# Self attentions of a four-layer decoder: keys and queries split and stacked through DRAM, one fp32r product of scores for four heads, half batches in one pipeline

## The chip, the core and the metric

The kernel is written for one NeuronCore of a Trainium2 chip. The metric is the device time of one execution in microseconds (us), as the median of several executions. The engines are named as in the profile: PE is TensorE (its weight loads are PEld), DVE is VectorE, ACT is ScalarE, POOL is GpSimd, and SP is SyncE, which issues the DMAs.

## What is computed

A decoder of four layers works on 16 batches of 100 tokens with 128 features; each layer is a self attention, a cross attention over 1444 context rows and a feed-forward block. The change concerns the four self attentions alone. Layer 1's is the plainest:

```python
q, k, v = split(x @ w_attn.T)                 # 16 heads of 8 features each
att = einsum('bhqd,bhkd->bhqk', q, k) / sqrt(8)
att = where(causal, att, -inf); att = softmax(att)
y = einsum('bhqk,bhkd->bhqd', att, v)
x = x + y @ w_proj.T
```

Layer 0 has biases, a temperature of 0.1 and a gate for each token, a clipped sigmoid that multiplies the attention's output. Layer 2 is a differential attention: two softmaxes a head (q1, k1 and q2, k2), whose outputs are subtracted with a factor lambda, values 16 wide, an RMS norm for each head, and no causal mask. Layer 3 divides the 8 features of each head of q and of k by their norm before the scores.

## The kernel before

x lies in SBUF with features on the 128 partitions and the 1600 tokens in the free dimension; xn is its layer norm. There are four groups of four batches (`NG`, `GB`; `GT` is 400 tokens). Each engine has a program of its own, in the order of the stages: self attention, cross attention and feed-forward, with layer norms between them. The order within an engine is that of the code; engines wait for each other by semaphores.

`self_attention(n)` loops over the four groups, and the loop's turns do not overlap. Each turn has three parts.

First the preparation: DVE copies the group to `xg` (L1552), PE makes q and k for 400 tokens in fp32 (L2509), ACT copies them to `qk`, and PE makes the values (L2526 adds the bias row, L2527 is the product), which ACT writes to `vaug` with a column of ones beside each head. A head has 8 of the 128 partitions, so for the scores the keys are masked: `km` holds 16 copies of the keys, one for each head, with all other heads' features set to zero. ACT makes five of them, DVE nine and POOL two.

Then come 8 half batches (16 in layer 2), called steps below and numbered k. Each has 8 heads:

```python
scores(k)   # PE: two products; each 4 heads of masked keys (400 columns), fp32, 128 rows
shift(k)    # DVE: maximum over 8x100 (L1604), subtracted in two halves (L1609)
exp(k)      # ACT: L1077
turn(k)     # PE: 8 transposes of 100x100 (L2485); ACT copies them back (L1083)
values(k)   # PE: 8 products of 9 or 17 columns (L2498); every second k DVE divides by the sum
```

PE takes them in the order values(k-1), turn(k), scores(k+2). The causal mask is added by a bf16 product ahead of each fp32 product (L2473). The scores stand in two pairs of PSUM banks.

Last comes the group's end: four transposes of y (L2552), the output product (L2559), and the addition to x on DVE (L1684). Layer 2 has its RMS norm before that, with a square root on ACT (L1088).

SP has no part in a self attention before the change, so it has already asked for the next stage's weights and context.

Of the kernel before, what the change touches and what calls it, by code (L numbers as in the profile page):

```python
# [35 lines left out]
ACT_KEYS, DVE_KEYS = 5, 14  # L36
# [8 lines left out]
class Semaphores:  # L45

    def __init__(self, made):
# [23 lines left out]
        self.xg_ready = made("xg_ready")  # L71
        self.proj_full = made("proj_full")
        self.proj_free = made("proj_free")
        self.proj_even_free = made("proj_even_free")
        self.proj_odd_free = made("proj_odd_free")
# [4 lines left out]
        self.qk_ready = made("qk_ready")  # L80
        self.v_ready = made("v_ready")
        self.gate_ready = made("gate_ready")
# [77 lines left out]
        self.keys_ready = made("keys_ready")  # L160
        self.keys_there = made("keys_there")
        self.q_stack_free = made("q_stack_free")
        self.slot_free = made("slot_free")
        self.km_act = made("km_act")
        self.km_dve = made("km_dve")
        self.km_pool = made("km_pool")
# [167 lines left out]
def constants():  # L334
# [12 lines left out]
    head_of = (i[:, None] // 8 == np.arange(HEADS)[None, :]).astype(np.float32)  # L347
    return dict(ident=ident, mean=mean, ones=ones, causal=np.tile(causal, (1, 4)), row96=row96,
                own_head=own_head, head_rows=head_rows, head_of=head_of,
# [5 lines left out]
def build(nc, dram, where, out):  # L355
# [31 lines left out]
    proj_bank_free = [s.proj_even_free, s.proj_odd_free]  # L387
# [32 lines left out]
    xg = shared([128, GT])  # L420
    qk = shared([128, 4, GT])
    km = shared([128, 2 * HEADS, GT])
    vaug = shared([S, GB, 16 * 17])
    gate = shared([S, GB])
# [4 lines left out]
    y_tok = shared([S, GB, 256])  # L429
    y_sq = shared([S, GB, 256])  # L430
    y_rms = shared([S, GB * 16])
    y_feat = shared([128, 2, GT])
# [4 lines left out]

    def rounded(name, shape, at):

        return nc.alloc_sbuf_tensor_at(name, shape, F32R, offset=at)  # L440
# [15 lines left out]

    def rounded_in_arena(name, shape):
        filled[0] = -(-filled[0] // 8) * 8
        at = arena_at + 4 * filled[0]
        filled[0] += math.prod(shape[1:])  # L460
        assert filled[0] <= ARENA, filled
        return rounded(name, shape, at)
# [28 lines left out]
    q_dram = nc.dram_tensor("q_dram", (2, 128, B, S), F32).ap()  # L491
# [103 lines left out]

    CHUNKS = [(0, 482), (482, 962), (962, K)]
# [76 lines left out]
    def _(sp):  # L673
# [8 lines left out]
        def self_attention(n):  # L682
            pass
# [176 lines left out]
    def _(pool):  # L860
# [3 lines left out]
        def self_attention(n):  # L864
            nsm = SELF[SA[n]]["nsm"]
            pool.wait_ge(loaded["const"], 16)
            with pool.Fori(0, NG) as g:
                for sm in range(nsm):
                    pool.wait_ge(s.keys_ready, 1)
                    pool.sem_inc(s.keys_ready, -1)  # L870
                    for h in range(DVE_KEYS, HEADS):
                        ins = nc.gpsimd.tensor_scalar(km[:, HEADS * sm + h, :], qk[:, 2 * sm + 1, :],  # L872
                                                      W("const", "head_of")[:, h:h + 1], None, ALU.mult)
                    ins.then_inc(s.km_pool, 1)
# [134 lines left out]
    def _(act):  # L1009
# [11 lines left out]
        def self_attention(n):  # L1021
            cfg = SELF[SA[n]]
            nsm, vw = cfg["nsm"], cfg["vw"]
            if cfg.get("diff"):
# [8 lines left out]
            with act.Fori(0, NG) as g:  # L1033
                for m in range(2 * nsm):
                    act.wait_ge(s.proj_full, 1)
                    act.sem_inc(s.proj_full, -1)
                    if cfg["bias"]:
                        ins = nc.scalar.activation(qk[:, m, :], bank(6 - m % 2), ACT.Identity, bias=W(SA[n], "bqk")[:, m:m + 1])
                    else:
                        ins = nc.scalar.activation(qk[:, m, :], bank(6 - m % 2), ACT.Copy)  # L1040
                    ins.then_inc(s.act_done, 1)
                    act.wait_ge(s.act_done, 1)
                    act.sem_inc(s.act_done, -1)
                    act.sem_inc(proj_bank_free[m % 2], 1)
                    if cfg.get("unit"):
                        nc.scalar.activation(group(squares, 0), bs(qk[:, m, :]), ACT.Square).then_inc(s.head_sq, 1)
                        act.wait_ge(s.head_norm, 1)
                        act.sem_inc(s.head_norm, -1)
                        nc.scalar.activation(group(deviation, 0), bs(bank(7)), ACT.Sqrt).then_inc(s.head_dev, 1)
                        act.wait_ge(s.unit_done, 1)  # L1050
                        act.sem_inc(s.unit_done, -1)
                    if m % 2 == 1:
                        act.sem_inc(s.keys_ready, 1)
                        act.sem_inc(s.keys_there, 1)
                for b in range(GB):
                    act.wait_ge(s.proj_full, 1)
                    act.sem_inc(s.proj_full, -1)
                    v = vaug[:, b, 0:16 * (vw + 1)].rearrange("p (h w) -> p h w", w=vw + 1)
                    nc.scalar.activation(v[:, :, 0:vw], bank(6 - b % 2, 16 * vw, S).rearrange("p (h w) -> p h w", w=vw), ACT.Copy).then_inc(s.act_done, 1)
                    act.wait_ge(s.act_done, 1)  # L1060
                    act.sem_inc(s.act_done, -1)
                    if cfg.get("gate"):
                        nc.scalar.activation(gate[:, b:b + 1], bank(6 - b % 2, 1, S, 128), ACT.Exp, scale=-1.0).then_inc(s.act_done, 1)
                        act.wait_ge(s.act_done, 1)
                        act.sem_inc(s.act_done, -1)
                    act.sem_inc(proj_bank_free[b % 2], 1)
                    act.sem_inc(s.gate_ready if cfg.get("gate") else s.v_ready, 1)
                for sm in range(nsm):
                    for h in range(ACT_KEYS):
                        ins = nc.scalar.activation(km[:, HEADS * sm + h, :], qk[:, 2 * sm + 1, :], ACT.Copy,  # L1070
                                                   scale=W("const", "head_of")[:, h:h + 1])
                    ins.then_inc(s.km_act, 1)
                N = GB * nsm * 2
                for k in range(N):
# [10 lines left out]
                if cfg.get("diff"):  # L1085
                    act.wait_ge(s.rms_sum, 1)
                    act.sem_inc(s.rms_sum, -1)
                    nc.scalar.activation(y_rms[:, :], y_rms[:, :], ACT.Sqrt, bias=eps_col(0)[0:S]).then_inc(s.rms_root, 1)  # L1088
                for c in range(cfg["vw"] // 8):
                    act.wait_ge(s.y_turned, 1)  # L1090
                    act.sem_inc(s.y_turned, -1)
# [2066 lines left out]
```

## Time and profile before

| | |
|---|---|
| median of 3 runs | 6973.69 us (6966.38 to 6979.26) |
| the profiled execution: its time | 6992.31 us |
| its span in the trace | 6989.8 us |
| self attention of layer 0, from 49.7 to 317.4 us | 267.7 us |
| self attention of layer 1, from 2035.3 to 2289.3 us | 254.0 us |
| self attention of layer 2, from 2781.4 to 3293.6 us | 512.2 us |
| self attention of layer 3, from 4647.8 to 5010.1 us | 362.3 us |
| the four together | 1396.2 us |

The bounds of the four are read from the timeline: the start is the end of the layer norm (or of layer 1's rounding of weights, or layer 2's batch norm), and the end is the last addition to x. A time in the timeline is the start of a group of equal instructions, followed by how long the group took. PE's ends are modelled, so distances between starts are more exact than durations. An fp32 product is shown as two instructions (x2 for one product). PEclk is the granted TensorE clock: 1.00 is 2.4 GHz and 0.50 is 1.2 GHz, and there is no level between them; a stretch's mean lies between.

### The profile page before, as it was taken

To read this page: it belongs to the slowest core of one execution; us is meant where nothing else is said; L and a number is where in the kernel's file an instruction comes from. 1 tells how busy PE (TensorE), PEld (TensorE's weight loads), DVE (VectorE), ACT (ScalarE), POOL (GpSimd) and SP (SyncE) were. 2 spreads that over 40 slices of the span, in tenths; PEclk is the share of its full clock that TensorE was granted. 3 is DMA by queue.
4 is the path that set the end of the run, shared out by engine and by line. 5 is a ranking of instruction groups with operands and counts; after the bars stand their busy time and mean duration, and the time that the engine had idled before them with its cause. 6 is when DMAs were issued, how large, how long until landed. Compare 5 with 4: busy or idle time off the path is not lost. (4 is left out here: it accounts for less than half of the span.)

```text
span 6989.8 us, 84197 instructions
## 1 busy us (share of the span) xinstructions
PE 5342.1 (76%) x22438; PEld 3563.2 (51%) x22438; DVE 3721.6 (53%) x5691; ACT 2289.8 (33%) x3467; POOL 1660.6 (24%) x1011
## 2 busy tenths in 40 slices
PE   6799999998977666776788888846667666764488
PEld 4578888785445543554455555524433333442244
DVE  4344444443444224444666666453377777776544
ACT  2255555552223112332455555422211111110122
POOL 0055665551000000000566666400000000000000
PEclk7689999997987667666898999766555555555689
DMA  1000000000110112000211121000000000000011
GB/s 60 0 7 21 14 14 14 16 13 19 39 30 0 45 45 58 0 0 1 57 41 40 39 46 39 18 0 0 14 11 15 13 13 13 13 17 0 0 39 41
DMA packets 124882, 151.26 MB, mean 22 GB/s; under 512 B 87408, under 2 KB 110720, under 8 KB 124448
## 3 DMA queue, kind: packets, MB, share of 16 engines
q1 hardware_dynamic: 124576, 147.90, 8.9%
q8 instruction: 104, 1.70, 0.1%
q14 instruction: 202, 1.65, 0.1%
HBM read 109.50 MB, written 2.66 MB: 16 GB/s over the span
## 5 line engine op out<-in xcount | busy, mean ns | idle before, releaser
L971 POOL TENSOR_TENSOR pexp_lo<-arena,pexp_hi 128x800 fp32r<-128x800 f32 x384 | 727.1, 1894 | 443.0 <-POOLq L970 442.0
L926 POOL TENSOR_TENSOR pexp_lo<-arena,pexp_hi 128x800 fp32r<-128x800 f32 x384 | 637.8, 1661 | 470.1 <-POOLq L925 470.1
L1978 DVE TENSOR_REDUCE arena<-ps 100x1 f32<-100x482 f32 (+1 forms) x768 | 477.7, 655 | 235.6 <-DVEq L1947 216.9
L1833 DVE TENSOR_REDUCE arena<-ps 128x1 f32<-128x482 f32 (+3 forms) x624 | 392.8, 656 | 387.9 <-DVEq L1811 373.0
L3005 PE MATMUL ps<-arena 100*128 100x100 f32 (+1 forms) x1536 | 338.1, 420 | 322.4 <-PEq L3001 322.4
L872 POOL TENSOR_SCALAR arena<-arena,w_const 128x400 f32<-128x400 f32 x40 | 59.5, 1498 | 1878.2 <-POOLq L870 1878.2
L3005 PEld LDWEIGHTS ps<-arena 100*128 100x128 f32 (+1 forms) x1536 | 323.1, 318 | 356.1 <-issue 356.1
L1169 ACT ACTIVATE arena<-ps 128x800 f32<-128x800 f32 x384 | 322.1, 839 | 513.2 <-ACTq L1167 511.2
L1235 ACT ACTIVATE arena<-ps 128x800 f32<-128x800 f32 x384 | 321.6, 837 | 431.4 <-ACTq L1229 377.6
L2860 PE MATMUL ps<-kst,qs 96*100 96x482 f32 (+1 forms) x768 | 338.8, 442 | 115.4 <-PEq L2820 111.2
L2257 DVE MATCH_REPLACE8 arena<-arena 100x1444 f32<-100x1444 f32 x256 | 421.6, 1647 | 0.0
L2475 PE MATMUL ps<-arena 128*100 128x400 f32 x640 | 353.8, 664 | 26.3 <-PEq L2536 26.3
L998 POOL TENSOR_SCALAR arena<-arena 1x1444 bf16<-1x1444 uint8 x16 | 81.0, 5063 | 1202.0 <-POOLq L996 1202.0
L2993 PE MATMUL ps<-ctxT,arena 96*100 96x482 f32 (+1 forms) x384 | 362.4, 1046 | 0.0
L2498 PEld LDWEIGHTS ps<-arena 100*100 100x100 f32 x2560 | 312.8, 204 | 77.2 <-issue 77.2
L3100 PE MATMUL ps<-arena,chunk 128*128 128x400 f32 x648 | 285.5, 522 | 73.1 <-PEq L3099 72.5
L2254 DVE MAX8 arena<-arena 100x8 f32<-100x1444 f32 x192 | 319.9, 1666 | 30.1 <-DVEq L2259 4.5
L1170 ACT ACTIVATE pexp_hi<-ps 128x800 fp32r<-128x800 f32 x384 | 319.5, 832 | 0.0
L1236 ACT ACTIVATE pexp_hi<-ps 128x800 fp32r<-128x800 f32 x384 | 319.4, 832 | 0.0
L2498 PE MATMUL ps<-arena 100*100 100x9 f32 (+1 forms) x2560 | 301.7, 258 | 9.6 <-PEq L2495 6.8
L2360 DVE TENSOR_TENSOR arena<-ps,arena 128x400 f32<-128x400 f32 x256 | 146.9, 574 | 294.2 <-DVEq L2351 183.0
L1282 ACT ACTIVATE arena<-ps 100x482 f32<-100x482 f32 (+1 forms) x192 | 95.6, 571 | 604.5 <-ACTq L1280 604.5
(350 smaller groups left out, 10874.1 us busy)
## 6 DMA issues: line engine op xcount, KB each, us to landing
ctxT<-in_ctxT SPq DMA_DIRECT2D x64, 541.5 KB
ctxk<-in_ctx SPq DMA_DIRECT2D x48, 528.0 KB
kst<-mid SPq DMA_DIRECT2D x128, 180.5 KB, 3.1
chunk<-in_ff_chunks SPq DMA_DIRECT2D x77, 193.0 KB, 2.4
arena<-gate_dram SPq DMA_DIRECT2D x64, 200.0 KB, 3.2
kst<-xn SPq DMA_DIRECT2D x64, 180.5 KB, 2.9
arena<-gate_dram SPq DMA_DIRECT2D x64, 100.0 KB, 2.6
w_cross<-in_ca SPq DMA_DIRECT2D x1, 3728.5 KB, 12.6
```

The source lines that it names most:

```text
L926: own(nc.gpsimd.tensor_tensor(pexp_lo[p % 3][:, :, :], pexp[p % 3], pexp_hi[p % 3][:, :, :], ALU.subtract))
L971: own(nc.gpsimd.tensor_tensor(pexp2_lo[p % 3][:, :, :], pexp2[p % 3], pexp2_hi[p % 3][:, :, :], ALU.subtract))
L1169: nc.scalar.activation(pexp[p % 3], of, ACT.Exp, scale=scale).then_inc(s.pexp_ready, 1)
L1235: nc.scalar.activation(pexp2[p % 3], of, ACT.Exp, scale=scale).then_inc(s.pexp_ready, 1)
L1833: peak = nc.vector.tensor_reduce(mparts[0:at.stop - at.start, m, c:c + 1], bank(k, z - a, at.stop - at.start), AX.X, ALU.max)
L1978: peak = nc.vector.tensor_reduce(mparts2[:, h, c:c + 1], bank(k, z - a, S), AX.X, ALU.max)
L2257: nc.vector.match_replace(left, top8[:, r, :], sc if r == 0 else left, TAKEN).then_inc(s.dve_done, 1)
L2475: last = mm(bank(2 * (k % 2) + c, GT, S), qk[:, 2 * sm, b * S:b * S + S], km[:, h:h + 4, b * S:b * S + S], start=not cfg["causal"], stop=True)
L2498: last = mm(bank(7, vw + 1, S, h * (vw + 1)), probsT[:, k % 2, c * GT + j * S:c * GT + j * S + S], vaug[:, b, h * (vw + 1):(h + 1) * (vw + ...
L2860: ins = mm(bank(k, z - a, S), qs[par][0:C, g, S * (h % 4):S * (h % 4) + S], kst[0:C, g, a:z], start=True, stop=True)
L2993: ins = mm(to, qv[:, h, :], ctxT[par][0:C, a:z], start=False, stop=True)
L3005: ins = mm(bank(6, S, r, t % 4 * S), kept[:, h, 128 * t:128 * t + r], turn_scale[:, h, :], start=h == 0, stop=h == TH - 1)
```

## The change

Projections come first, for all 1600 tokens. Each of q and k is written as two fp32r parts, high and low, to `staged`; SP stores them in DRAM (`heads_dram`) and loads them again as stacks of 96 rows: `q_rows` holds, for groups of four heads, the 32 features three times (high, low, high), and `k_diag` holds four heads' keys on a block diagonal (high, high, low), with zeros between, that POOL has set. One fp32r product of 96 rows gives the scores of four heads; the masked copies `km` are gone. `k_diag`'s second buffer shares its memory with `staged`.

The rest is units of 8 steps: four batches in layers 0, 1 and 3 (4 units), two in layer 2 (8 units). A unit has its own stack, loaded while the unit before it runs. The steps run on from unit to unit: the values of the next unit, and the transposes, output product and update of the previous one, stand between the steps (`VALUES_AT`, `TURNS_AT`). PE's order in a step is turn(k), scores(k+2), values(k-1). DVE subtracts the maximum in one instruction, and with no bias adds to x from PSUM directly. Layer 2's root is asked for once per unit, so 8 times where there were 4.

```diff
+    VALUES_AT = {1: (0, 1, 2, 6), 2: (0, 1)}
+    TURNS_AT = {1: (3,), 2: (3, 4)}
+    def all_units(nsm, unit):
+        for u in range(4 * nsm):
+            unit(u, u % 2, u == 0, u == 4 * nsm - 1)
...
@@ SP: self_attention @@
+            def load(u, par):
+                at = slice(cols * u, cols * u + cols)
+                for sm in range(nsm):
...
+                    for r, part in enumerate((0, 1, 0)):
+                        of = heads_dram[4 * sm + part, :, at].rearrange("(g d) t -> d g t", g=4)
+                        sp.dma_start(q_to[32 * r:32 * r + 32, sm].bitcast(F32), of).then_inc(stack_loaded[sm][par], 16)
+                    for j in range(4):
+                        for r, part in enumerate((2, 2, 3)):
+                            of = heads_dram[4 * sm + part, :, at].rearrange("(g j d) t -> j d g t", g=4, j=4)
+                            sp.dma_start(k_to[32 * r + 8 * j:32 * r + 8 * j + 8, sm, :, j].bitcast(F32),
+                                         of[j]).then_inc(stack_loaded[sm][par], 16)
+            def reload(u, par):
+                sp.wait_ge(s.q_stack_free, 1)
...
+            for m in range(2 * nsm):
+                sp.wait_ge(s.heads_split, 1)
...
+                for part in range(2):
+                    sp.dma_start(heads_dram[2 * m + part], staged[m % 2][part].rearrange("p b t -> p (b t)")).then_inc(s.scratch_stored, 16)
+                if m % 2 == 1:
+                    sp.wait_ge(s.scratch_stored, 64)
...
+                    sp.sem_inc(s.staging_free if m + 1 < 2 * nsm else s.zeros_asked, 1)
...
+            load(0, 0)
...
+            load(1, 1)
+            for u in range(2, 4 * nsm):
+                reload(u, u % 2)
@@ POOL: self_attention @@
-                    for h in range(DVE_KEYS, HEADS):
-                        ins = nc.gpsimd.tensor_scalar(km[:, HEADS * sm + h, :], qk[:, 2 * sm + 1, :],
+            nc.gpsimd.memset(k_diag[0][:, :].bitcast(F32), 0.0).then_inc(s.row_ones, 1)
+            pool.wait_ge(s.zeros_asked, 1)
...
+            nc.gpsimd.memset(k_diag[1][:, :].bitcast(F32), 0.0).then_inc(s.row_ones, 1)
@@ DVE: self_attention @@
+            for m in range(2 * nsm):
+                for g in range(NG):
+                    hi, lo = [group(t.bitcast(F32R), g) for t in staged[m % 2]]
+                    if cfg.get("unit"):
...
+                        done(nc.vector.tensor_scalar(norm, norm, 1e-8, None, ALU.max))
+                        done(nc.vector.reciprocal(norm, norm))
+                        done(nc.vector.tensor_tensor(raw, raw, norm, ALU.mult))
+                        done(nc.vector.tensor_copy(hi, raw))
+                        done(nc.vector.tensor_tensor(lo, raw, hi, ALU.subtract))
...
+            def shift(k):
...
+                done(nc.vector.tensor_reduce(mx, sc, AX.X, ALU.max))
+                done(nc.vector.tensor_tensor(sc, sc, mx.unsqueeze(3).to_broadcast([S, 2, 4, S]), ALU.subtract))
...
+            def unit(u, par, first=False, last=False):
+                for k in range(8):
+                    shift(k)
+                    if k == 7 and not last:
+                        dve.sem_inc(s.q_stack_free, 1)
+                    if k in (4, 6):
+                        normalise(k // 2 - 2, par)
+                    if not first and k in (0, 2):
+                        normalise(k // 2 + 2, 1 - par)
+                    if not first and k == 2:
+                        finish(1 - par)
+                    if not first and k == 7:
+                        update(u - 1)
@@ PE: self_attention @@
-                    last = mm(bank(2 * (k % 2) + c, GT, S), qk[:, 2 * sm, b * S:b * S + S], km[:, h:h + 4, b * S:b * S + S],
-                              start=not cfg["causal"], stop=True)
+                    last = mm(bank(2 * (k % 2) + c, GT, S), q[:, sm, g, at], keys[:, sm, g, :, at], start=not cfg["causal"], stop=True)
...
+            def unit(u, par, first=False, last=False):
+                for k in range(8):
+                    turn(k, first and k == 0)
+                    if k < 6:
+                        scores(k + 2, par)
+                    elif not last:
+                        scores(k - 6, 1 - par)
                     if k > 0:
-                        values(k - 1)
+                        values(k - 1, par)
+                    elif not first:
+                        values(7, 1 - par)
+                    if k in VALUES_AT[nsm] and not last:
+                        value_rows(u + 1, VALUES_AT[nsm].index(k))
+                    if not first and k in TURNS_AT[nsm]:
+                        features(1 - par, k - TURNS_AT[nsm][0])
+                    if not first and k == 5:
+                        project()
```

On PE one step in the middle of a group of layer 0 stood so before the change, with the values of the step before, the eight transposes, and then the scores, each causal product followed by the product of four heads (the weights are `qk`, the columns `km`, both in `arena`):

```order
L2498 MATMUL ps<-arena 100x9 x8
L2485 MATMUL ps<-w_const,arena 100x100 x8
L2473 MATMUL ps<-causal_bf,ident_bf 100x400
L2475 MATMUL ps<-arena 100x400
L2473 MATMUL ps<-causal_bf,ident_bf 100x400
L2475 MATMUL ps<-arena 100x400
```

In the changed kernel the second step of the first unit of layer 0 stands so, again on PE:

```order
L2568 MATMUL ps<-w_const,arena 100x100 x8
L2555 MATMUL ps<-causal_bf,ident_bf 100x400
L2556 MATMUL ps<-k_diag_51,q_rows_49 100x400
L2555 MATMUL ps<-causal_bf,ident_bf 100x400
L2556 MATMUL ps<-k_diag_51,q_rows_49 100x400
L2584 MATMUL ps<-arena 100x9 x8
L2539 MATMUL ps<-w_sa,w_const 100x128
L2540 MATMUL ps<-w_sa,xn 100x128
```

The scores moved ahead of the values, their operands are the two stacks, and one batch's values for the next unit follow. All else in a step is as many instructions as before.

SP's program went in layer 0 from the last of the small weights straight to the cross attention's weights and context:

```order
L677 DMA w_ff<-in_ff 128x16
L697 DMA w_cross<-in_ca 128x7457
L688 DMA ctxT<-in_ctxT 96x1444
L689 DMA ctxk<-in_ctx 128x11x96
L691 DMA ctxk<-in_ctx 36x96
```

In the changed kernel the stores and the four loads of stacks stand between, and this repeats in each of the other three layers (with twice as many per unit and eight units in layer 2):

```order
L689 DMA w_ff<-in_ff 128x16
L722 DMA heads_dram<-arena 128x1600 x4
L706 DMA q_rows_49<-heads_dram 32x4x400 x3
L710 DMA k_diag_51<-heads_dram 8x4x400 x12
L706 DMA q_rows_50<-heads_dram 32x4x400 x3
L710 DMA k_diag_52<-heads_dram 8x4x400 x12
L706 DMA q_rows_49<-heads_dram 32x4x400 x3
L710 DMA k_diag_51<-heads_dram 8x4x400 x12
L706 DMA q_rows_50<-heads_dram 32x4x400 x3
L710 DMA k_diag_52<-heads_dram 8x4x400 x12
L748 DMA w_cross<-in_ca 128x7457
```

The cross attention's weights and first context moved behind the last stack, which SP can issue only when DVE has shifted the last scores of unit 1.

## Rows read from the trace of the kernel before

**Rows 1.** Windows, one for each self attention: busy us of each engine (instructions), PEclk, DMA.

```profile
49.70:317.40 267.70, 196.11 (x1064) 137.11 (x1064) 108.87 (x208) 85.80 (x164) 12.30 (x8) 0.72 0.00 0
2035.30:2289.30 254.00, 188.65 (x1032) 133.78 (x1032) 102.28 (x181) 82.34 (x148) 11.52 (x8) 0.72 0.00 0
2781.40:3293.60 512.20, 374.21 (x1904) 269.60 (x1904) 232.87 (x388) 163.78 (x284) 23.93 (x16) 0.68 0.00 0
4647.80:5010.10 362.30, 231.07 (x1080) 154.25 (x1080) 131.15 (x204) 101.42 (x172) 11.75 (x8) 0.63 0.00 0
```

**Rows 2.** Timeline of layer 0: first group's start, last group's end (start, us, what).

```profile
51.83 0.37 DVE L1552 COPY arena<-xn 128x400 f32 x1 [0.52 <-DVEq L1548]
...
66.77 0.54 PE L2473 MATMUL ps<-causal_bf,ident_bf 100*100 100x400 bf16 x1 [4.71 <-PEq L2536]
...
74.18 0.87 PE L2485 MATMUL ps<-w_const,arena 100*100 100x100 f32 x8 [1.99 <-PEq L2481]
...
306.39 1.54 PE L2485 MATMUL ps<-w_const,arena 100*100 100x100 f32 x8 [2.06 <-PEq L2481]
...
316.77 0.57 DVE L1684 TENSOR_TENSOR x<-x,squares 128x400 f32 x1 [0.22 <-DVEq L1678]
```

**Rows 3.** Timeline of PE, layer 1, a stretch at PEclk 1.00.

```profile
2247.23 1.50 PE L2498 MATMUL ps<-arena 100*100 100x9 f32 x16
2248.58 0.87 PE L2485 MATMUL ps<-w_const,arena 100*100 100x100 f32 x8
2249.29 0.33 PE L2473 MATMUL ps<-causal_bf,ident_bf 100*100 100x400 bf16 x1
...
2250.98 1.50 PE L2498 MATMUL ps<-arena 100*100 100x9 f32 x16
```

**Rows 4.** Timeline of PE, layer 2, a stretch at PEclk 0.50.

```profile
2983.91 2.74 PE L2498 MATMUL ps<-arena 100*100 100x17 f32 x16
2986.49 1.55 PE L2485 MATMUL ps<-w_const,arena 100*100 100x100 f32 x8
2987.84 2.87 PE L2475 MATMUL ps<-arena 128*100 128x400 f32 x4
2990.50 2.74 PE L2498 MATMUL ps<-arena 100*100 100x17 f32 x16
```

**Rows 5.** Windows around stretches of either level, columns as in rows 1.

```profile
2982.20:2999.20 17.00, 17.00 (x73) 12.87 (x72) 4.99 (x8) 4.19 (x7) 0.00 (x0) 0.50 0.00 0
...
138.80:156.00 17.20, 14.45 (x108) 10.92 (x107) 10.50 (x17) 6.94 (x12) 0.00 (x0) 1.00 0.00 0
```

**Rows 6.** Timeline of PE, cross attention of layer 0: fp32r products at PEclk 0.50.

```profile
373.31 0.54 PE L2734 MATMUL ps<-qa_lo,ctxT_hi 113*128 113x400 f32 x1
373.64 0.54 PE L2735 MATMUL ps<-qa_hi,ctxT_lo 113*128 113x400 f32 x1
```

**Rows 7.** Timeline, layer 0: DVE's shift of one step, and one bias product of values on PE.

```profile
302.68 0.99 DVE L1604 TENSOR_REDUCE arena<-ps 100x8 f32<-100x800 f32 x1 [0.35 <-DVEq L1601]
303.82 1.31 DVE L1609 TENSOR_TENSOR ps<-ps,arena 100x400 f32<-100x400 f32 x2
...
125.50 0.75 PE L2526 MATMUL ps<-w_sa,w_const 1*100 1x129 f32 x2
```

**Rows 8.** Timeline, cross attention of layer 2: stores to DRAM, stacks loaded, first product of them.

```profile
3319.30 0.43 SPq L767 DMA_DIRECT2D q_dram<-deviation  x1
3324.32 4.11 SPq L733 DMA_DIRECT2D qs<-q_dram  x12
...
3333.52 0.69 PE L2860 MATMUL ps<-kst,qs 96*100 96x482 f32 x1 [8.18 <-PEq L2820]
```

**Rows 9.** Layer 3's reciprocal on DVE; layer 2's table load on ACT; a memset on POOL.

```profile
4659.41 2.65 DVE L1564 RECIPROCAL deviation<-deviation 128x400 f32<-128x400 f32 x1
...
3025.26 1.28 ACT L1088 ACT_TABLE_LOAD   x1 [7.34 <-ACTq L1087]
...
L978 POOL MEMSET qs<- 100x1600 f32 x2 | 2.9, 1431 | 131.1 <-POOLq L976 131.0 <-POOLq L962 0.2
```

More of the change, by code:

```diff
@@ L1032, in self_attention, with heads @@
             act.sem_inc(s.stage_act, -1)
[L1033 to L1046, printed above, removed]
+            def heads(to, m, g):
+                act.wait_ge(s.proj_full, 1)
+                act.sem_inc(s.proj_full, -1)
+                of = bs(bank(4 * (m % 2) + g))
+                if cfg["bias"]:
+                    own(nc.scalar.activation(group(to, g), of, ACT.Identity, bias=W(SA[n], "bqk")[:, m:m + 1]))
+                else:
+                    own(nc.scalar.activation(group(to, g), of, ACT.Copy))
@@ L1068, in self_attention @@
[L1068 to L1074, printed above, removed]
+                        nc.scalar.activation(group(deviation, g), bs(bank(4 * (m % 2) + g)), ACT.Sqrt).then_inc(s.head_dev, 1)
+                else:
+                    for g in range(NG):
+                        heads(staged[m % 2][0].bitcast(F32R), m, g)
+                        act.sem_inc(s.heads_hi, 1)
@@ L1688, in self_attention @@
+            if cfg.get("diff"):
+                done(nc.vector.tensor_scalar(subln[:, :], W(wst, "subln")[0:S, :], 1 - LAMBDA_INIT, None, ALU.mult))
+            all_units(nsm, unit)
+            normalise(2, 1)
+            normalise(3, 1)
+            finish(1)
+            update(4 * nsm - 1)
+            dve.wait_ge(s.q_stack_free, 1)
+            dve.sem_inc(s.q_stack_free, -1)
             dve.sem_inc(s.stage_pe, 1)
@@ L2466, in self_attention @@
             wqk, wv, wo = W(wst, "wqk"), W(wst, "wv"), W(wst, "wo")
-            N = GB * nsm * 2
-            def scores(k):
-                b, sm, half = k // (2 * nsm), k // 2 % nsm, k % 2
+            per = 4 // nsm
+            for m in range(2 * nsm):
+                for g in range(NG):
+                    if m > 1:
+                        pe.wait_ge(s.heads_read, 1)
+                        pe.sem_inc(s.heads_read, -1)
+                    mm(bank(4 * (m % 2) + g), wqk[:, m * 128:m * 128 + 128], group(xn, g), start=True, stop=True).then_inc(s.proj_full, 1)
+                if cfg.get("unit"):
+                    for g in range(NG):
+                        pe.wait_ge(s.head_sq, 1)
+                        pe.sem_inc(s.head_sq, -1)
+                        mm(bank(4 * (m % 2) + g), W("const", "head_rows"), group(squares, g), start=True, stop=True).then_inc(s.head_norm, 1)
@@ L2562, in cross_single @@
+            for i in range(per):
+                value_rows(0, i)
+            scores(0, 0)
+            scores(1, 0)
+            all_units(nsm, unit)
+            pe.wait_ge(s.probsT_ready, 2)
+            pe.sem_inc(s.probsT_ready, -2)
+            values(7, 1)
+            for c in range(nsm):
+                features(1, c)
+            project()
         def cross_single():
```

491 lines of the change are left out of this document (225 added, 266 removed).

## The prediction, made before the changed kernel ran

> **What bounds the kernel now.** I read the page first: its slices show that the four self attentions are spread over the span, with PE far from full in each. Then the windows of each: 267.7, 254.0, 512.2 and 362.3 us, 1396.2 together, at PEclk 0.72, 0.72, 0.68 and 0.63 [rows 1]. The rest of the kernel, 5594 us, is the same code after the change. The reader should see that no engine is full: in layer 0 PE is busy 196 of 268 us and DVE 109 [rows 1].
>
> The timeline says why. A group of layer 0 begins at 51.83 and its first score product at 66.77, its first transposes at 74.18; the last transposes start at 306.39 and x is done at 317.34 [rows 2]. So of each group's 67 us (267.7/4) some 33 are preparation, filling and emptying, and 8 steps share the rest: 306.39 - 74.18 is 232 us for four groups less three turns of about 33, which leaves 132 us for 28 steps, 4.7 us each.
>
> A step's price depends on the clock. At 1.00 the values start at 2247.23, the transposes at 2248.58, the scores at 2249.29 and the next values at 2250.98: 1.35 + 0.71 + 1.69 = 3.75 us [rows 3]. At 0.50 in layer 2, which has no causal products, it is 2.58 + 1.35 + 2.66 = 6.59 us [rows 4], so an fp32 product of 400 columns is 1.33 us. PE is then the bound: busy 17.0 of 17.0 us [rows 5].
>
> **The scores.** An fp32r product of 400 columns starts 0.33 us after the one before at the low level [rows 6]; the fp32 one takes four times that. The causal product, one pass over 400 columns, takes 0.33 too. At the low level a step is then 1.35 (turn) + 4 x 0.33 (scores) + 2.58 (values) = 5.25 us; layer 2 with no causal products has 4.6. At the high level it is 0.71 + 0.68 + 1.35 = 2.75.
>
> **What stands between the steps.** A pair of instructions for the values takes about 0.7 us at the low level [rows 7]: with a bias 1.36 a batch, four batches in 8 steps, 0.7 a step; without it 0.35; in layer 2, with twice the columns, 0.25. The output product (1.33) and four transposes (0.67) add 0.25. Sums at the low level: 6.2 us a step in layers 0 and 3, 5.9 in layer 1, 5.1 in layer 2.
>
> **DVE and ACT beside it.** The maximum starts at 302.68 and the subtraction at 303.82; two subtractions take 1.31 [rows 7]. One of 800 columns should take what the maximum over 800 takes, 0.99. With 0.35 of handover the shift is 2.5 us; dividing by the sum and the update to x make it 3.2 a step. ACT has less. So at the low level DVE hides behind PE's 5 to 6 us, and the one subtraction saved earns nothing. If PE ran at the high level, that cover would be gone and DVE's 3.2 us would stand level with PE's 3.2 to 3.4.
>
> **The clock.** This decides the size. The granted clock rose in the stretch from 138.80, 1.00 for 17 us, right after four fp32 score products in a row; it fell after values and transposes with few columns. And it stayed at 0.50 for 17 us in which PE was busy 17.0 us, four-pass products among them [rows 5]. The change takes three of four passes out of the only long streams of a step. I conclude that PE will be full and at the low level: 6.2 us steps, longer than the 4.7 of today. A short rise should follow the output product, the one four-pass product left in a unit; I take 0.1 us off each step for it, so 6.1, 5.8 and 5.0. The Trainium skill says otherwise: in "TensorE: Matmul & The Clock Gate", section "What's actually happening", the hardware sets the clock "based on how busy the PE has been recently". By that rule a PE that never pauses runs at the high level, and the time would be the third rival's; the 17 busy us at 0.50 speak against it.
>
> **Preparation, now once per layer.** Eight fp32 projections at 1.33 are 10.7 us; with the table load ahead of the first copy and the last copy and subtraction, 13. From the second store's issue to the first load's is 5.0 us, and from the first of 12 stack loads and three key loads to the first product 9.2 us [rows 8]; the new load is also 15 DMAs. So layer 1 takes 13 + 0.4 + 5 + 9.2 = 28 us. Layer 0's gate products (64 instructions of 0.17, 10.7 us), the gate's exponential and four batches of values (2 us each) run beside the DMAs but are longer: 33 us. Layer 2 splits two pairs, with a store between (staging is reused), and loads 30 DMAs: 13 + 5.4 + 8 + 5.4 + 14.3, about 47. In layer 3 DVE has a reciprocal of 2.65 us [rows 9] and four passes of some 0.65 with gaps for each of 8 groups, 5.3 each; ACT's roots wait for the first half to end, which puts 8.6 ahead of the first and 4 between: 8.6 + 21 + 4 + 21 + 5.4 + 9.2, 70 us. POOL's memsets are 1.43 us for 1600 columns [rows 9], 5.7 for 6400, behind the projections and the first load; uncovered they would cost those 5.7 us a layer.
>
> **Filling and emptying.** 74.18 - 66.77 is 7.4 us, less 2.0 for two short products: 5.4. The end takes 317.34 - 306.39 = 10.9 as now, less 1.3 in the last steps, which have no scores. Layer 2 needs 4.7 and, with its RMS norm, 17.
>
> **The new wait.** In layer 2 `finish` makes DVE wait for ACT's root inside step 2, and ACT comes to it after the copies of turn(2). Behind it on DVE stands shift(3), on which turn(3) waits. After turn(2) come copies 0.6, table load 1.28 [rows 9], root and handover 0.4, reciprocal and two multiplications 2.0, shift 2.5, the table of Exp again 1.28, exp 1.2: 9.1 us and turn(2)'s own 1.35, against a step of 5.1. PE loses 5.3 us in seven of eight units, 37 us.
>
> **The sum.**
> Layer 0: 33 + 5.4 + 31 x 6.1 - 1.3 + 10.9 = 237.
> Layer 1: 28 + 5.4 + 31 x 5.8 - 1.3 + 10.9 = 223.
> Layer 2: 47 + 4.7 + 63 x 5.0 - 0.7 + 37 + 17 = 420.
> Layer 3: 70 + 5.4 + 31 x 6.1 - 1.3 + 10.9 = 274.
> Together 1154 instead of 1396, 242 less. The profiled execution took 6992.3, so it would take 6750; the median of the runs lies 18.6 under it, which gives 6732, and I say 6733. What moved behind the last stack load on SP (weights of 3.7 MB and the context) is issued when unit 1 ends, with two units of nearly 50 us still to run; I cost it at nothing. Uncovered, it would cost its landing, some 13 us in layer 0.
>
> **The rivals.**
> First, a mixed clock. If PE is at the high level for the share of time of today (0.72 is 44 in 100), steps are 4.6, 4.4 and 4.3 us instead of 6.1, 5.8 and 5.0: 45 + 43 + 44 + 45, some 180 us less, 6553. For it: rows 1, and output product and transposes follow each other. Against: what raises the clock has gone from the other steps. Chance 13 in 100.
>
> Second, stack loads slower than rows 8 shows: 12 of 15 DMAs write 8 partitions only. At 1 to 1.6 us for each, instead of 0.34, first loads and layer 2's units (30 DMAs against about 31 us of cover) lose 50 to 200 us: 6780 to 6930. Chance 10 in 100.
>
> Third, PE at the high level throughout: steps of 3.5, 3.3 and 3.3 us with DVE level with PE, and 7 us for each root: 157 + 145 + 320 + 194 = 816, so 580 less, 6394. The rows of either level speak for it only where four-pass products stand close. Chance 8 in 100. The rule of the Trainium skill quoted above leads here.
>
> Fourth, slower than before, by the same DMAs. With L us for 15 of them, layers 0, 1 and 3 lose L - 9 each at the start, layer 2 loses 2L - 14 there and 2L - 31 in each of six later units. At L = 28, that is 1.9 us a DMA, this eats all 242 us. At 2.5 us it is 7135. 12 DMAs were issued in 4.11 us [rows 8], with chunks of 400 bytes instead of 1600. Chance 4 in 100. No change to be measured, where these losses just cancel, 2 in 100.
>
> **How the numbers follow.** My own case holds 63 in 100, with 6660 to 6800 as its range. 6540 to 6850 leaves out the third and fourth rivals (12), a part of the mixed clock (5) and the end of the slow loads (3). Faster by over 0.2% (14 us, what a measurement of this kernel can tell) is all but the fourth and the cancelling: 94; same 2, slower 4.
>
> **What would show it.** PEclk near 0.5 in the four windows with PE busy over 90% in the units; 16 values products about 2.6 us apart from the transposes; steps near 6.1 us; the first transposes of layer 0 some 38 us after its start, of layer 3 some 75; one gap of 5 us on PE per unit of layer 2, ended by the exp; no wait of PE for the stacks after the first. A PEclk over 0.7, or waits of PE for stack loads between units, would make the prediction wrong, in opposite directions.

## The result and the profile after

The change made the kernel faster, by less than half of what was predicted: 6877.69 us (6870.09 to 6891.85, 4 runs) against 6976.48 us for the kernel before in the same runs, a ratio of 0.9846 [0.982, 0.9872]. The prediction was 6733 us (6540 to 6850), a ratio of 0.966. The direction was right, the size was not, and the time lies outside the range. The profiled span is 6890.1 us, 99.7 less than before.

First the page, busy time of each engine and the slices with the granted clock. The clock's digits are lower than before in the slices that hold the self attentions (the first two, 7 and 6 before, are now 5 each; so are the 13th and 14th, the 17th to 19th and the 28th):

```profile
PE 5319.9 (77%) x22198; PEld 3730.9 (54%) x22198; DVE 3622.7 (53%) x5355; ACT 2229.9 (32%) x3354; POOL 1643.6 (24%) x979
PEclk5589999997985577555899999865555555555689
```

Then the windows of the four self attentions, which answer to [rows 1]. The column after the five busy times is PEclk:

```profile
50.00:317.00 267.00, 222.19 (x1064) 194.88 (x1064) 84.02 (x116) 71.21 (x126) 10.72 (x2) 0.51 0.23 54
2037.00:2292.00 255.00, 197.77 (x968) 174.87 (x968) 80.41 (x109) 68.97 (x125) 10.65 (x2) 0.51 0.21 42
2783.00:3272.00 489.00, 343.58 (x1793) 311.98 (x1794) 195.26 (x274) 156.06 (x263) 10.77 (x2) 0.52 0.13 38
4610.00:4915.50 305.50, 217.13 (x1016) 183.95 (x1016) 114.69 (x145) 77.57 (x141) 10.86 (x2) 0.52 0.12 28
```

Together 1316 us (to the tenth, by the last additions to x, 1315.4), where 1396.2 stood and 1154 was forecast. Layers 0 and 1 gained nothing at all, layer 2 gained 24 us, layer 3 57 us. The clock is where the prediction put it, 0.51. But PE is busy 222 of 267 us, not over 90% of the time.

The timeline of layer 1 shows why. One step, from one group of transposes (L2568) to the next; the lines are those of the kernel after. L2555 is the mask product, L2556 the fp32r score product, L2584 the values of the half batch before, L2540 the value projection of the next unit, L1155 ACT's copies of the transposes, L1128 its copy of the projected values, L1149 the exponential:

```profile
2133.19 1.54 PE L2568 MATMUL ps<-w_const,arena 100*100 100x100 f32 x8 [1.89 <-PEq L2564]
...
2134.53 0.54 PE L2555 MATMUL ps<-causal_bf,ident_bf 100*100 100x400 bf16 x1
...
2134.86 0.50 ACT L1155 ACTIVATE arena<-ps 100x400 f32<-100x400 f32 x1 [0.16 <-ACTq L1154]
...
2135.87 2.72 PE L2584 MATMUL ps<-arena 100*100 100x9 f32 x16
...
2137.36 1.00 DVE L1667 TENSOR_TENSOR ps<-ps,arena 100x800 f32<-100x800 f32 x1
2138.43 0.73 PE L2540 MATMUL ps<-w_sa,xn 128*100 128x128 f32 x2
2139.29 0.28 ACT L1128 ACTIVATE arena<-ps 100x128 f32<-100x128 f32 x1 [3.92 <-ACTq L1124]
2139.92 0.84 ACT L1149 ACTIVATE arena<-ps 100x800 f32<-100x800 f32 x1 [0.35 <-ACTq L1148]
2141.05 1.54 PE L2568 MATMUL ps<-w_const,arena 100*100 100x100 f32 x8 [1.89 <-PEq L2564]
```

The shift is done at 2138.36, and ACT has been free since 2135.36. Yet the exponential starts at 2139.92: ahead of it in ACT's queue stands the copy of the projected values, idle for 3.92 us until PE's last work of the step (2138.43) is done. PE then waits 1.89 us for the exponential, since all that stands in its queue comes behind these transposes. So the step takes 7.86 us where 5.25 + 0.7 = 5.9 were meant to do.

That is the rule, not an exception. The waits ahead of the transposes, for all four layers:

```profile
its engine sat idle before it (us, times) until:
  issue: 239.2, 102
  PEq L2564: 189.1, 80
```

L2564 is the last of PE's waits ahead of the transposes: 189 us in 80 steps. Seven of them are the root steps of layer 2 with 6.42 us each, 45 us, which have another cause (experiments 4 and 6); the other 73 have 1.89 to 2.31 us each. By the timeline it is the exponential that ends them; the copies of the step before were done long ago.

Set beside the prediction's terms, from the starts in the timeline (four layers in turn; the steps are the time from the first to the last transposes):

| | measured | forecast |
|---|---|---|
| start to first transposes | 39.0, 38.4, 47.9, 80.7: 206 us | 38.4, 33.4, 51.7, 75.4: 199 us |
| steps | 214.1, 203.7, 420.3, 210.9: 1049 us | 187.8, 178.5, 351.3, 187.8: 905 us |
| from the last transposes | 13.8, 12.7, 20.4, 13.5: 60 us | 10.9, 10.9, 17, 10.9: 50 us |

144 of the 161 us that are missing are in the steps. The rest of the kernel took 5575 us in place of 5594, some 20 less.

### The profile page after: what moved, and what is told of

Same layout as the page of the kernel before. It is cut to its first block and busy times, and to the rows that moved or that the text cites. A ratio compares the mean times of both kernels' runs of the same rounds, so it can differ in the third digit from the quotient of the medians.

```text
span 6890.1 us, 83173 instructions
## 1 busy us (share of the span) xinstructions
PE 5319.9 (77%) x22198; PEld 3730.9 (54%) x22198; DVE 3622.7 (53%) x5355; ACT 2229.9 (32%) x3354; POOL 1643.6 (24%) x979
## 5 line engine op out<-in xcount | busy, mean ns | idle before, releaser
L2584 PEld LDWEIGHTS ps<-arena 100*100 100x100 f32 x2560 | 458.8, 285 | 17.7 <-issue 4.1
L1666 DVE TENSOR_REDUCE arena<-ps 100x8 f32<-100x800 f32 x160 | 158.7, 992 | 550.0 <-DVEq L1663 550.0
L2584 PE MATMUL ps<-arena 100*100 100x9 f32 (+1 forms) x2560 | 432.3, 313 | 2.7 <-PEq L2576 2.7
L2568 PE MATMUL ps<-w_const,arena 100*100 100x100 f32 x1280 | 246.1, 373 | 201.5 <-PEq L2564 189.1
L2568 PEld LDWEIGHTS ps<-w_const,arena 100*100 100x100 f32 x1280 | 209.1, 207 | 240.1 <-issue 239.2
```

Of the source, the lines that this page charges most:

```text
L2568: last = nc.tensor.transpose(bank(4 + c, S, S, j * S), probs[:, k % 2, at:at + S], ident[0:S, 0:S])
L2584: last = mm(bank(7, vw + 1, S, h * (vw + 1)), probsT[:, k % 2, c * GT + j * S:c * GT + j * S + S], vaug[:, par, at:at + vw + 1], start=Tru ...
```

## The experiments

The columns of this table are the median, the ratio to the kernel before in the same runs with its 95% interval, and the steps of the four layers in the profiled execution as above. Small differences are better read from the ratios, since the kernel before had medians of 6975 to 6994 us in the different groups of runs. The profiled execution isn't the median one: it took 7111.67 us in 2, 6721.56 in 3, 6590.79 in 5, 6577.86 in 7 and 6700.89 in 9. The diffs are shortened; indices and some waits are left out.

| | us | ratio | steps: layers 0, 1, 2, 3 |
|---|---|---|---|
| after | 6877.69 | 0.9846 [0.982, 0.9872] | 214, 204, 420, 211 |
| 1 ACT's order | 6698.78 | 0.9588 [0.9548, 0.9628] | 178, 160, 356, 178 |
| 2 four-pass scores | 7055.06 | 1.009 [1.0061, 1.0119] | 249, 258, 487, 253 |
| 3 both | 6656.06 | 0.9506 [0.9467, 0.9545] | 150, 124, 416, 167 |
| 4 root early on ACT | 6875.57 | 0.9832 [0.9798, 0.9866] | 214, 204, 403, 211 |
| 5 ACT's order, four-pass but in layer 2 | 6619.73 | 0.9502 [0.9444, 0.956] | 144, 125, 356, 149 |
| 6 ACT's and DVE's order | 6689.78 | 0.9582 [0.9529, 0.9636] | 178, 160, 334, 181 |
| 7 as 6, four-pass but in layer 2 | 6586.53 | 0.9455 [0.9403, 0.9506] | 150, 125, 334, 144 |
| 8 as 6, mask product four times | 6592.70 | 0.9458 [0.9403, 0.9514] | 148, 125, 334, 145 |
| 9 as 6, three times | 6670.23 | 0.954 [0.9508, 0.9571] | 180, 147, 334, 181 |
| 10 as 6, twice | 6735.86 | 0.9641 [0.9605, 0.9676] | 185, 167, 334, 198 |
| 11 as 7, four-pass in layer 2 too | 6633.65 | 0.9505 [0.9463, 0.9548] | 144, 124, 353, 150 |
| 12 as 6, values in their own step | 7050.10 | 1.0079 [1.004, 1.0117] | 242, 232, 483, 243 |

**1. ACT's order.** The copies of a step's side products go behind the next step's exponential; PE and DVE are untouched.

```diff
     exp(k)
+    if k - 1 in VALUES_AT[nsm] and not last: value_rows(...)
+    if not first and k - 1 in TURNS_AT[nsm]: features(...)
     copies of turn(k)
-    if k in VALUES_AT[nsm] and not last: value_rows(...)
-    if not first and k in TURNS_AT[nsm]: features(...)
```

> Edit: on ScalarE the copies of a step's side products (the next unit's values, the transposed features) come after the next step's exponential instead of before it; nothing else. Theory A (the queue of ScalarE): TensorE's waits of 1.9 to 2.4 us ahead of the transposes are there because exp(k+1) stands behind a copy that itself waits for the last product of step k. Then the 7.9 and 8.7 us steps become 5.9 and 6.6, the waits of TensorE ahead of the transposes go from 189 us to under 60 in sum, and the time falls by about 150 us to some 6730. Theory B (the wait is for the copies of the transposes or for the handover of the side bank): no change, 6878. For the clock: if the low level came from these pauses, the granted clock rises well over 0.6 in the four stages and the time falls below 6600; if it comes from what TensorE streams, it stays at 0.50 to 0.55.

6698.78 us, 179 less than after; the steps of the profiled execution shrank by 177 us (871.5 in place of 1049). A step with a value projection takes 5.8 us in layer 1 and 6.5 in layer 0, and the first theory stands: PE's waits at L2564 fell from 189.1 to 45.4 us, which are the root steps. The same kind of step in layer 1, 5.77 us from the transposes at 2105.17 to the next; the exponential for the transposes at 2110.94 has started at 2107.25, the copy L1128 comes behind both, and PE's rows have no idle time:

```profile
2105.17 1.55 PE L2568 MATMUL ps<-w_const,arena 100*100 100x100 f32 x8
...
2107.25 0.83 ACT L1149 ACTIVATE arena<-ps 100x800 f32<-100x800 f32 x1
...
2107.85 2.72 PE L2584 MATMUL ps<-arena 100*100 100x9 f32 x16
...
2110.42 0.73 PE L2540 MATMUL ps<-w_sa,xn 128*100 128x128 f32 x2
...
2110.94 1.54 PE L2568 MATMUL ps<-w_const,arena 100*100 100x100 f32 x8
...
2111.28 0.28 ACT L1128 ACTIVATE arena<-ps 100x128 f32<-100x128 f32 x1 [3.20 <-ACTq L1124]
```

**2. Four-pass scores.** The stacked score product as fp32 instead of fp32r, in the changed kernel as it is. It then takes four passes over its columns instead of one, and a plain step 7.2 us instead of 5.25.

```diff
-    mm(..., q[:, sm, g, at], keys[:, sm, g, :, at], ...)
+    mm(..., q[:, sm, g, at].bitcast(F32), keys[:, sm, g, :, at].bitcast(F32), ...)
```

> Edit: the score product reads the same stacks as fp32, four passes instead of one; nothing else, so each step streams more columns. Theory C (the level follows what TensorE streams): the granted clock in the four stages rises from 0.51 to over 0.75, plain steps take about 3.8 us instead of 5.25 although their product has four passes, steps with side work about 6.4, and the time falls by 200 to 280 us, to some 6600 to 6680. Theory D (the level follows pauses and busy time alone): the clock stays near 0.5, each step takes 2.0 us more, and the time rises by about 300 us to some 7180.

7055.06 us: neither. The clock rose only a little, to 0.52 to 0.58 over the steps of a layer. Windows of the steps of layers 0 and 1:

```profile
91.30:340.50 249.20, 219.01 (x975) 162.95 (x976) 72.10 (x96) 60.89 (x108) 0.00 (x0) 0.58 0.14 35
2116.10:2374.60 258.50, 229.41 (x951) 173.02 (x952) 69.12 (x91) 60.22 (x108) 0.00 (x0) 0.52 0.11 20
```

PE still stood still 1.9 to 2.2 us ahead of the transposes in the steps with a projection or `features`, and most steps ran at the low level at 7.2 to 10.7 us.

**3. Both.**

> Both edits, the order of ScalarE and the four-pass product. Theories A and C together: steps near 3.8 to 4.4 us at a granted clock over 0.85, the stage of layer 0 about 180 us instead of 267, time some 400 us under the changed kernel, about 6470. If D holds: 7180 less what the order gives, about 7030. If B and C hold: as with the four-pass product alone, 6600 to 6680.

6656.06 us: better than either alone, not as good as expected. Four-pass products cost 177 us on the kernel after, and gain 43 us once ACT's order is mended. Layers 0 and 1 reached the high level (150 and 124 us), but in layer 2 the root step still took 10.9 to 11.2 us and the clock fell behind it: 416 us, 60 more than with fp32r. In ratios the gain is 0.8%, and the intervals of 1 and 3 all but touch.

**4. Root early on ACT.** The root step is the one in a unit of layer 2 in which DVE waits for ACT's square root; it takes 11.2 us in the kernel after. Here ACT takes the root right behind exp(2), ahead of the copies of turn(2).

```diff
     exp(k)
+    if not first and k == 2: root()
     copies of turn(k)
-    if not first and k == 2: root()
```

> Edit: in layer 2 ScalarE takes the square root right after exp(2) instead of after the copies of the transposes of step 2; layers 0, 1 and 3 are as in the changed kernel. My account of the step of 11.2 us (VectorE waits for the root, and shift(3) and the transposes of step 3 for VectorE): the step falls to about 5 to 6 us in seven units, layer 2 by 40 to 46 us, time about 6835. Rival: the step is long for VectorE's own work in the norm (squares, sums, two multiplications, 4 to 5 us), then it falls by 1 to 2 us only and the time by 10 us.

No change that can be measured (6875.57 against 6877.69 us). The root step did shrink, from 11.2 to 8.7 us, and layer 2's steps with it from 420 to 403 us. But the way from its last transposes to layer 3's first took 1453.1 us in place of 1439.5, which is the same code. Neither theory had that.

**5 to 8. The two orders and the clock.** In 6, DVE's part of the RMS norm is cut in two; shift(3) goes between:

```diff
     if not first and k == 2: finish(1 - par)        # squares and their sums; rms_sum
+    if not first and k == 3: finish_rest(1 - par)   # wait for the root; reciprocal, two multiplications
```

5 and 7 have the four-pass product only in layers 0, 1 and 3 (`nsm == 1`). 8 keeps fp32r and writes the mask four times over:

```diff
-    mm(bank(...), ident_bf[0:S, 0:S], causal_bf[:, :], start=True, stop=False)
+    for _ in range(4):
+        mm(bank(...), ident_bf[0:S, 0:S], causal_bf[:, :], start=True, stop=_ < 3)
```

> ACT's order as in the first experiment, and the fp32 score products (four passes) in layers 0, 1 and 3 only. Theory: once ACT's order no longer makes PE wait, the additional passes lift the granted clock in these three layers by more than they cost. From first to last transposes the kernel with ACT's order alone took 178, 160 and 178 us there, the one with both changes 150, 124 and 167, so 6699 - 28 - 36 - 11 = 6624 us, with layer 2 at 356 us as with ACT's order alone. Rival: where the clock rises depends on what the execution did before, and another execution with the same code in these layers keeps 0.5 there; a step then grows by 2 us to 7.2 and more, and the time is over 6800 us.

> ACT's order as in the first experiment; in layer 2 DVE's wait for the root and what follows it stand behind shift(3) instead of ahead of it. Theory: the 11.2 us of the root step are DVE's order: shift(3) stands behind the wait for the root. With shift(3) ahead, exp(3) waits only for ACT's two table loads and the root (1.28 + 0.32 + 1.28 us), and the step shrinks to about 6 us: 7 times 5 us less than ACT's order alone, 6699 - 35 = 6664 us. Rival: ACT's own work sets the step (copies, table, root, table, exp), since moving the root ahead of the copies left the total where it was; then the step stays over 9 us and the time over 6685 us.

> Both orders (ACT's copies behind the next exp, DVE's root behind shift(3)) and four-pass products in layers 0, 1 and 3. Theory: the effects add, 6699 - 75 - 35 = 6589 us. Rival: what is saved in layer 2 is given back as a lower clock in the stages behind it, as it was when the root was moved on ACT (layer 2's steps took 18 us less, and the stages from its end to layer 3's first transposes 14 us more); then about 6610 us.

> Both orders, the score product in fp32r, and in layers 0, 1 and 3 the bf16 product of the causal mask made four times (the same bank written anew each time), so that PE streams as many columns in a step as with four-pass products. Theory A: what lifts the clock is the streaming, whatever the type: clock and time as with four-pass products, 6589 us. Theory B: it is the fp32 products, and bf16 ones don't lift it: the clock stays at 0.5, a step takes 2 us more, and the time is 6664 + 93 x 2 = 6850 us.

5: 6619.73 us, expected 6624. 7: 6586.53 us, expected 6589. 6: 6689.78, which the intervals can't tell from experiment 1 (6698.78). Its mechanism is in the trace, though. The root step takes 6.3 us, not 11.2, and the step behind it 6.7 instead of 4.9: 3.1 us a unit, 22 us in layer 2 (334 in place of 356), not 35. Most of what the step behind it lost is a new wait: DVE's rest of the norm now stands ahead of shift(4) and of the division (L1679) that frees the output bank, and PE waits 1.48 us for it ahead of its values (L2592). In that execution the way from layer 1's last transposes to layer 2's first took 578 us, as in 3 and 8 to 12 (575 to 578); in 1, 2, 4, 5, 7 and the kernel after it was 550 to 555. This is code that no experiment touches, with a granted clock of 0.65 in place of 0.71, and it gave back the 22 us: the profiled executions of 1 and 6 took 6702.55 and 6703.23 us. Between 5 and 7, whose profiled executions are both on the short side, DVE's order brought 33 us in the medians but 13 us between the two profiled executions, and the intervals of the ratios overlap. So what DVE's order is worth in the whole time isn't shown; in layer 2 it is 22 us.

The timeline of the root step in 6 and of the wait behind it (here L1160 is the copies, L1143 the root, L1701 what waits for it, L2576 the transposes). ACT goes from the copies to the exponential by two table loads, and DVE's shift is long done:

```profile
2808.78 1.10 ACT L1160 ACTIVATE arena<-ps 100x400 f32<-100x400 f32 x2 [0.35 <-ACTq L1159]
...
2809.89 1.28 ACT L1143 ACT_TABLE_LOAD   x1
2811.19 0.32 ACT L1143 ACTIVATE arena<-arena,eps 100x32 f32<-100x32 f32 x1
2811.53 1.28 ACT L1149 ACT_TABLE_LOAD   x1
2811.66 0.35 DVE L1701 RECIPROCAL arena<-arena 100x32 f32<-100x32 f32 x1 [4.39 <-DVEq L1700]
...
2812.82 0.84 ACT L1149 ACTIVATE arena<-ps 100x800 f32<-100x800 f32 x1
...
2813.96 1.54 PE L2576 MATMUL ps<-w_const,arena 100*100 100x100 f32 x8 [1.52 <-PEq L2572]
...
2816.93 0.42 DVE L1679 TENSOR_TENSOR arena<-ps,arena 100x256 f32<-100x256 f32 x1
...
2817.65 2.82 PE L2592 MATMUL ps<-arena 100*100 100x17 f32 x16 [1.48 <-PEq L2584]
```

8 gave 6592.7 us, the same as four-pass products: theory A. The bf16 mask product has no fp32 work in it, and lifts the clock as well. The windows of the steps of 6, then of 8:

```profile
90.10:268.10 178.00, 178.00 (x915) 163.71 (x916) 72.09 (x96) 59.44 (x108) 0.00 (x0) 0.51 0.20 49
2026.20:2186.00 159.80, 158.30 (x891) 148.24 (x891) 69.14 (x91) 58.05 (x108) 0.00 (x0) 0.55 0.19 33
2764.00:3098.00 334.00, 310.36 (x1704) 294.11 (x1705) 176.63 (x243) 140.89 (x238) 0.00 (x0) 0.52 0.12 30
```

```profile
91.90:239.80 147.90, 147.57 (x1094) 126.78 (x1094) 72.30 (x97) 57.09 (x108) 0.00 (x0) 0.86 0.25 59
2005.00:2130.40 125.40, 124.91 (x1071) 110.33 (x1072) 69.39 (x92) 55.60 (x108) 0.00 (x0) 0.98 0.23 40
2705.40:3039.60 334.20, 310.56 (x1704) 294.35 (x1705) 176.66 (x243) 140.90 (x238) 0.00 (x0) 0.52 0.12 30
```

In 6 PE is busy 178.00 of 178.00 us in layer 0, and the clock is 0.51. In 8 it is as full, with more work in each step, at 0.86, and 30 us shorter. PE's busy time in the profile is thus no sign of the clock.

**9 and 10. Fewer mask products.**

> Both orders, fp32r scores, the causal product three times instead of four in layers 0, 1 and 3. At the high level a step is then 0.71 + 2 x 4 x 0.17 + 1.35 = 3.4 us instead of 3.75, and DVE's shift with the division by the sum, 3.2 us a step, still fits. If the granted clock stays as high as with four (0.77 over the kernel), some 93 steps save 0.33 us each: 6593 - 31 = 6562 us. Rival: the additional columns were just enough, and with fewer of them the clock goes back to 0.5 in part of the layers; then a plain step is 5.25 + 4 x 0.33 = 6.6 us there, and the time lies between 6600 and 6750 us.

> The same with the causal product twice. If the clock stayed high, a step would be bounded by DVE's 3.2 us or PE's 3.1, and the time 6593 - 50 = 6543 us. I expect the rival here: with once it is 0.5, and with twice PE streams a third of what four times adds, so the clock falls back to 0.5 and steps are 5.9 us: 6664 + 93 x 0.67 = 6726 us, or up to 6750.

With the mask product once, twice, three and four times the kernel takes 6690, 6736, 6670 and 6593 us, and layer 0's PEclk is 0.51, 0.56, 0.63 and 0.86. Both went the rival's way: twice is a loss, since the steps get longer and the clock hardly moves (46 us in the medians; the intervals of once and twice just overlap, but the steps of the three layers took 30 us more). Three times leaves layers 0, 1 and 3 in part at the low level (PEclk 0.63, 0.77 and 0.63; in layer 0 steps of 4.2 and of 6.6 to 7.9 us side by side).

**11. Four passes in layer 2 too, with DVE's order.**

> Both orders and four-pass products in all four layers, so layer 2 too. Theory: what kept layer 2's clock low with four-pass products (416 us from first to last transposes) was the root step, where PE stands still for several us a unit; with DVE's order PE is nearly always busy and the clock stays at 1.0: 63 steps of some 4.0 us, 255 us against 333 with fp32r products, so 6587 - 80 = 6507 us. Rival: the root step still drops the clock in each unit, steps are 6.6 to 7.5 us in most of it, layer 2 takes some 400 us and the time is 6587 + 65 = 6650 us.

6633.65 us, layer 2's steps 353 us at PEclk 0.69. Without DVE's order they took 416 (experiment 3), so the root step had been one thing that dropped the clock. It still drops in each unit: in most of them steps of 3.4 to 5.4 us up to the root, and 6.7 to 8.0 behind it. Against 7 (334 us) it does not pay.

**12. One part of the change undone.** The values of a half batch behind its own transposes, not a step later; PE's wait for the copies moves with them, from ahead of the transposes to ahead of the values.

```diff
     turn(k)
     scores(k + 2)
-    values(k - 1)
+    values(k)
```

> Both orders as before (fp32r scores, one causal product), and one part of the change undone: the values of a half batch follow its own transposes in the same step, behind scores(k+2), instead of a step later. Theory: at the low level the copies of a turn end some 2.2 us after its start and the two scores at 2.7 us, so in layers 0, 1 and 3 nothing is lost; in layer 2, without causal products, the scores end at 2.0 us and PE waits 0.2 to 0.4 us in each of 64 steps: 10 to 25 us more than the kernel with both orders (6690), about 6705 us. Rival: the lag of a step is what keeps PE fed, also where ACT does the side copies first; PE then waits 1 us or more in each step, and the time is above 6780 us.

7050.1 us, 360 more, in the rival's way, but not by its mechanism: the copies were in time, as the theory had it. The timeline in layer 1 (here L2589 is the values, L1679 DVE's division by the sum):

```profile
2143.26 0.26 DVE L1676 RECIPROCAL arena<-ps 100x16 f32<-100x16 f32 x1 [0.35 <-DVEq L1673]
2143.67 0.29 DVE L1679 TENSOR_TENSOR arena<-ps,arena 100x128 f32<-100x128 f32 x1
2144.38 2.74 PEld L2589 LDWEIGHTS ps<-arena 100*100 100x100 f32 x16 [4.33 <-issue]
2144.41 2.81 PE L2589 MATMUL ps<-arena 100*100 100x9 f32 x16 [3.78 <-PEq L2584]
```

The outputs have one bank, free again when DVE has divided, and the division stands behind shift(k) in DVE's queue, which is placed for values one step later. PE waits 3.8 us here, and much the same in every second step: 30 times and 109 us in layers 0 and 1. So this run prices the lag together with DVE's unchanged order; with the division moved ahead it could cost less, which was not tried.

## Why the prediction was right and wrong

- **What failed: "ACT has less."** The prediction laid ACT's load beside PE's, found it small, and took steps of 6.1, 5.8 and 5.0 us from PE's work alone. It never wrote down ACT's queue with its waits, though it did so for DVE in layer 2. The step that failed is the path of a step: in the order exp, copies, side copy, exp, the side copy waits for what PE does last in a step, and so ties the next exponential to the end of this one. Steps with a value projection took 8.7, 7.9 and 7.7 us in layers 0, 1 and 2, those with `features` 8.3 (7.1 in layer 2). Mending this alone gave 179 us (experiment 1) and 6698.78 us, a step sum of 871.5 us against the 905.4 forecast. So part of the miss was hidden by errors the other way. One of them is in the sum: the side work was counted in all 31 steps of layers 0, 1 and 3, while value projections stand in 12 of them, and with ACT's order mended these layers' steps took 515.6 us where 554.1 were forecast.
- **Right: plain steps.** 5.2 to 5.3 us at the low level and 4.6 in layer 2, where 5.25 and 4.6 were worked out. The short rise of the clock behind the output product, for which 0.1 us a step was taken off, some 16 us in all, hardly came: the steps ran at 0.50 to 0.51.
- **Right: the clock.** 0.51, on thin grounds: 17 us at 0.50 with PE full [rows 5] and the reading that long score products raise it. Experiments 7 and 8 bear that reading out: with more passes for the scores or the mask it was 0.84 to 0.98 in layers 0 and 1. The quoted rule of the Trainium skill ("TensorE: Matmul & The Clock Gate", section "What's actually happening") would have it high where PE never pauses; experiment 6 has 178 busy us of 178 at 0.51, so the measurement decides against reading "busy" as the profile's busy time. The same page, section "Part 4: PE-mode transpose", says that transposes don't count as busy for the clock in the same way. Each step has eight transposes, so that fits; but no run here takes the transposes out, so it is not shown. The values, 2.6 of the 5.25 us of a plain step, are a rival that no run takes out either; which of the two keeps the clock low stays open. With PE's waits mended the clock stayed low too, 0.51 to 0.55 in experiment 1.
- **Mis-sized: the root.** 5.3 us of stall a unit were forecast. The root step took 11.2 us, 6.6 over a plain one of 4.6 and 6.1 over the 5.1 that the forecast set against it. The two steps behind it took 7.1 each, but these are ACT's side copies again (4.9 each in experiment 1). The direction and the queue (shift(3) behind the wait) were right; experiment 6 confirms it, with 3.1 us a unit to be had.
- **Right in sum: preparation.** 206 us to the first transposes, 199 forecast. The first stack load was mis-sized: in layer 1 the loads are issued from 2054.47 on and the first product that waits for them starts at 2069.00, 14.5 us where 9.2 were forecast, though the 12 key-stack loads are issued in 4.42 us, near the 4.11 of [rows 8]. PE never waits for a stack later in a layer. So the slow loads of the second and fourth rivals cost about 5 us once in that layer, and nothing between units.
- **Small misses:** the ends, 60 us in place of 50, and the rest of the kernel, which was taken to be the same and got 20 us shorter. What moved behind the last stack load (in layer 0 the cross attention's weights were issued at 193.89 instead of 14.37) was put at nothing, and no loss from it is seen in that sum.

## What to carry to other kernels

Before taking a step's time from the fullest engine, write down every engine's queue for one step with what each instruction waits for: an engine that is a third full still sets the pace if a late input stands ahead of an urgent output. When the clock is at its low level with PE full, try more work on PE as well as less, but only after PE's waits are gone: four-pass products in all layers cost 177 us before that and gained 43 after (2, and 3 against 1), and without layer 2, where PE still waited, they gained 103 (7 against 6). Measure an edit in a stage by that stage's time as well as by the total, since unrelated stages can give back as much.

## What was not expected of the hardware

The best kernel found, 6586.53 us, does its scores in four passes where one would do; it is some 4% faster than the changed kernel (0.9455 / 0.9846 = 0.960). Writing a mask four times into the same bank has the same effect, 6592.7 us. And stages whose code is the same in all kernels differ by what ran ahead of them: from layer 1's last transposes to layer 2's first it is 550 to 555 us in some and 575 to 578 us in others. What decides between the two was not found.
